# Cross-attention and mixture of experts in one kernel: the expert table and the zero blocks made in attention's block, four score banks in its drain, and other last sums and stores

## The reference

```python
x = x + tanh(g_xattn) * attention(layernorm(x), context)   # 16 heads of 16
x = x + tanh(g_ffn) * ffn(layernorm(x))

def ffn(x):                      # 12 experts, the top 3 of each row
    probs = softmax(x @ Wr + br)
    top_vals, top_idx = top_k(probs, 3)
    ew = softmax(top_vals)
    for e in range(12):
        sel = top_idx == e;  cnt = sel.sum()
        w_e = sum(where(sel, ew, 0)) / max(cnt, 1)
        h = relu(x @ w1[e] + b1[e]) @ w2[e] + b2[e]
        out = out + sel.any(-1)[..., None] * (w_e * h)
    phi = sigmoid(relu(out.mean(axis=1) @ Wp1 + bp1) @ Wp2 + bp2)
    return out * (1 - 0.8 * (phi > 0.7))
```

## Time and profile before

| | us |
|---|---|
| median of 3 timed runs | 2294.24 |
| lowest, highest | 2290.15, 2294.42 |
| the profiled execution | 2282.05 |
| its span, first to last instruction | 2280.3 |

### The profile page before, as it was taken

How to read it: one execution, slowest core, us unless ns; L and a number is a source line. 1 busy time by engine, 2 the same in 40 slices (tenths; PEclk the granted TensorE clock), 3 DMA queues, 4 the chain that set the end, 5 groups by cost and what they waited for, 6 DMA issues and landing times. The chain is left out here.

```text
span 2280.3 us, 61866 instructions
## 1 busy us (share of the span) xinstructions
PE 2146.6 (94%) x23534; PEld 1870.1 (82%) x23534; DVE 1414.3 (62%) x3219; ACT 1162.3 (51%) x2765; POOL 803.2 (35%) x1200
## 2 busy tenths in 40 slices
PE   5899999999999999999999999999993799999994
PEld 4688888888888888888888888888872678888883
DVE  4777777777777777777777777777743111111114
ACT  1366666666666666666666666666651223333330
POOL 4323433433433433443343343344211133333331
PEclk9999999999999999999999999999986899999996
DMA  5555555555555555555555555555403686777775
GB/s 137 146 132 151 138 139 138 134 148 137 132 137 139 146 139 141 134 139 144 136 131 139 150 134 144 134 135 137 125 19 104 209 270 187 218 220 218 210 222 158
DMA packets 253683, 345.06 MB, mean 151 GB/s; under 512 B 90280, under 2 KB 170508, under 8 KB 253260
## 3 DMA queue, kind: packets, MB, share of 16 engines
q1 hardware_dynamic: 222716, 304.93, 50.2%
q0 software_dynamic: 20256, 23.21, 5.2%
q10 hardware_dynamic: 10416, 12.98, 1.7%
HBM read 155.83 MB, written 42.86 MB: 87 GB/s over the span
## 5 line engine op out<-in xcount | busy, mean ns | idle before, releaser
L569 DVE TENSOR_REDUCE max_part<-max_ps 100x1 f32<-100x512 f32 (+1 forms) x1536 | 994.7, 655 | 349.2 <-PE max_ps L809 325.2
L452 ACT ACTIVATE probs<-score_ps 128x400 f32<-128x400 f32 (+1 forms) x1536 | 753.6, 503 | 427.6 <-PE score_ps L792 419.5
L792 PE MATMUL score_ps<-q_stack,k_stack 97*128 97x200 f32 (+1 forms) x3072 | 618.4, 284 | 4.6 <-ACT probs L452 3.4
L809 PE MATMUL max_ps<-k_stack,q_stack 96*100 96x512 f32 (+1 forms) x1536 | 597.2, 389 | 10.1 <-DVE max_part L569 9.6
L792 PEld LDWEIGHTS score_ps<-q_stack,k_stack 97*128 97x128 f32 (+1 forms) x3072 | 476.0, 184 | 78.0 <-issue 32.8
L389 POOL TENSOR_TENSOR ctx_hi<-ctx_raw,zero_col 128x256 fp32r<-128x256 f32 (+1 forms) x384 | 213.3, 586 | 467.7 <-PE v_ps L823 427.4
L859 PE MATMUL pv_ps<-probs,v_ones 128*17 128x100 f32 x12288 | 307.5, 253 | 0.6 <-ACT probs L452 0.6
L859 PEld LDWEIGHTS pv_ps<-probs,v_ones 128*17 128x17 f32 x12288 | 261.9, 99 | 45.1 <-issue 37.5
L809 PEld LDWEIGHTS max_ps<-k_stack,q_stack 96*100 96x100 f32 x1536 | 257.2, 167 | 21.6 <-DVE max_part L569 16.3
L1222 ACT ACTIVATE hid<-h_ps,b_c 128x256 f32<-128x256 f32 x245 | 116.0, 474 | 311.3 <-PE h_ps L1378 311.3
L1122 POOL DMA_INDIRECT results_by_token<-y_t,slot x98 | 152.9, 1561 | 343.1 <-DVE y_t L1329 185.3
(11 more groups left out here) (186 smaller groups left out, 2289.5 us busy)
## 6 DMA issues: line engine op xcount, KB each, us to landing
k_stack<-k_hl SPq DMA_DIRECT2D x512, 128.0 KB, 2.6
w_raw<-in_w SPq DMA_DIRECT2D x98, 640.0 KB, 5.2
ctx_raw<-in_ctxT SPq DMA_DIRECT2D x64, 512.0 KB, 4.5
k_stack<-k_hl SPq DMA_DIRECT2D x512, 64.0 KB, 2.2
k_stack<-k_hl SPq DMA_DIRECT2D x256, 105.0 KB, 2.5
ctx_raw<-in_ctxT SPq DMA_DIRECT2D x32, 420.0 KB, 4.8
k_stack<-k_hl SPq DMA_DIRECT2D x256, 52.5 KB, 2.0
x_t<-rows_by_expert SPq DMA_DIRECT2D x49, 269.0 KB, 4.8
```

The lines of the kernel that those rows point to most:

```text
L452: act.activation(probs[0:tw, n % PROBS, :], score_ps[n % 2][0:tw, 0:UH * SQ], ACT.Exp, scale=SCALE).then_inc(exp_done, 1)
L569: dve.tensor_reduce(max_part[b % 2][:, h, j:j + 1], max_ps[m % 2][0:SQ, 0:CW[j]], AX.X, ALU.max).then_inc(max_read, 1)
L792: ins = pe.matmul(score_ps[n % 2][0:TW[i], 2 * SQ * p:2 * SQ * (p + 1)], k_stack[b % 2][:, 2 * u + p, 128 * i:128 * i + TW[i]], q_stack[b ...
L809: pe.matmul(max_ps[m % 2][0:SQ, 0:CW[j]], q_stack[b % 3][0:96, h // 2, SQ * (h % 2):SQ * (h % 2) + SQ], k_stack[b % 2][0:96, h // 2, k0[j] ...
```

## The change

- In `attention`, POOL sets `zero_rows`, `ones_wide` and two rows of numbers in slot 378, in the room of `ctx_raw`, which is read no more by then.
- ACT issues the clear of `results_by_token` in slot 384 of attention.
- From score number 4 * 365 on (`WIDE` = 385 is its slot) the scores go round four banks, `v_ps` and `k_ps` being the other two, and wait for the exponential of n - 4. From tile 366 on (`SINGLE`) the values are multiplied tile by tile, 16 matmuls (32 instructions) in every slot.
- At the end of attention's lists PE makes the totals in `small_ps`; DVE adds `base` (the first row of each region) and writes the pads, and then the rest of the table and `wexp`, in the room of `probs`. SP and ACT issue six clears each as soon as the pads are there. SP waits for all clears before the block ends.
- `experts` begins with the load of the first rows and weights.
- In the tail DVE sums four of a part's five rows by two additions (2 x 512 wide to `pair_sum`, then 256), and PE takes the fifth row straight from `res` with a matmul pair of its own. A DVE step is folded into its neighbours: phi's last column is now -0.8 * (phi > 0.7), and factor is (sum + 1) * gate.
- Final products and stores go in pieces of 1, 2, 4, 6, 6 and 6 rows a partition, no longer five of 5.

```diff
+WIDE = NT * (B - 1) + 13
+SINGLE = NT * (B - 2) + 6
...
+def visit_of(tile):
+    return tile // 2 if tile < SINGLE else SINGLE // 2 + tile - SINGLE
...
+        def clear_pads(eng, some):
+            eng.wait_ge(pad_ready, 1)
+            for e in some:
+                row = eng.value_load(table[0:1, 3 * TILES + e:3 * TILES + e + 1], min_val=0,
+                                     max_val=NE * REGION - RT)
+                eng.dma_start(xs[bass.ds(row, RT), :].rearrange("(r p) d -> p r d", p=128),
+                              zero_rows.unsqueeze(1).broadcast_to([128, RT // 128, XW])).then_inc(cleared, 16)
+
+        drain_banks = [score_ps[0], score_ps[1], v_ps, k_ps]
+
+        def banks_of(n):
+            return 2 if n < UH * (WIDE - AT_SCORE) + 4 else 4
+
+        def score_bank(n):
+            return score_ps[n % 2] if n < UH * (WIDE - AT_SCORE) else drain_banks[n % 4]
...
+            clear_pads(sp, range(0, NE, 2))
             sp.wait_ge(x1_stored, 16 * B)
+            sp.wait_ge(cleared, 16 * NE)
+            sp.wait_ge(res_cleared, 16)
...
+                if g == NT * B - 6:
+                    pool.wait_ge(ctx_split, NC * B)
+                    pool.memset(zero_rows, 0.0).then_inc(tail_consts, 1)
+                    pool.memset(ones_wide, 1.0).then_inc(tail_consts, 1)
...
+                if g == NT * B:
+                    act.wait_ge(tail_consts, N_TAIL)
+                    act.dma_start(results, zero_rows[:, 0:D].unsqueeze(1).broadcast_to(
+                        [128, SLOTS // 128, D])).then_inc(res_cleared, 16)
+            clear_pads(act, range(1, NE, 2))
...
+            dve.wait_ge(totals_done, 1)
+            step(dve.tensor_copy(totals, small_ps[:, 0:2 * NE]))
+            step(dve.tensor_tensor(pad[0:SQ, :], base[:], totals[0:SQ, 0:NE], ALU.add))
+            dve.tensor_copy(table[0:SQ, 3 * TILES:], pad[0:SQ, :]).then_inc(pad_ready, 1)
...
-                wait(pe, exp_done, n + 1 - 2)
+                if n == UH * (WIDE - AT_SCORE):
+                    pe.wait_ge(v_read, NT * B)
+                    pe.wait_ge(k_read, KD * NC * B)
+                wait(pe, exp_done, n + 1 - banks_of(n))
...
-                if b is None or last % 2 == 0:
+                if b is None or (last % 2 == 0 and NT * b + last < SINGLE):
                     return
+                first = last - 1 if NT * b + last < SINGLE else last
...
-                for i in (last - 1, last):
+                for i in range(first, last + 1):
...
+            pe.matmul(small_ps[:, 0:2 * NE], ones_wide, counts[:], start=True, stop=True).then_inc(totals_done, 1)
...
-                dve.tensor_reduce(part_sum[:, i, :], res[0][:, pieces[i], :].rearrange("p i d -> p d i"), AX.X,
+                s = pieces[i].start
+                dve.tensor_tensor(pair_sum[:, i], res[0][:, s:s + 2, :], res[0][:, s + 2:s + 4, :],
+                                  ALU.add).then_inc(pair_ready, 1)
+                dve.wait_ge(pair_ready, i + 1)
+                dve.tensor_tensor(part_sum[:, i, :], pair_sum[:, i, 0, :], pair_sum[:, i, 1, :],
                                   ALU.add).then_inc(part_ready, 1)
...
             for i in range(PARTS):
+                pe.wait_ge(res_in[i], 16 * COPIES)
+                for k in range(KD):
+                    pe.matmul(pool_ps[:, k * B:k * B + B], res[0][:, pieces[i].stop - 1, 128 * k:128 * k + 128],
+                              of_batch[:], start=(i == 0 and k == 0), stop=False, skip_group_check=True)
                 pe.wait_ge(part_ready, i + 1)
```

More of the change, by code:

```diff
@@ L133, in attention @@
         slot_of = sb("slot_of", [SQ, TOPK, NE])
+        counts = sb("counts", [SQ, 2 * NE])
         half = sb("half", [SQ, 1])
@@ L150, in attention @@
         probs = sb("probs", [128, PROBS, UH * SQ])
+        room = probs[:].rearrange("p n q -> p (n q)")
+        totals, tmp, pad, ntiles, ends = (room[:, 32 * i:32 * i + n] for i, n in enumerate((2 * NE, NE, NE, NE, NE)))
+        t_exp, t_before, t_valid, t_row = (room[:, 192 + 64 * i:192 + 64 * i + TILES] for i in range(4))
+        more = room[:, 512:512 + NE * NCMP].rearrange("p (e c) -> p e c", e=NE)
+        past = room[:, 1024:1024 + TILES * NE].rearrange("p (t e) -> p t e", t=TILES)
+        skipped = room[:, 2048:2048 + TILES * NE].rearrange("p (t e) -> p t e", t=TILES)
         x_in = sb("x_in", [SQ, D])
@@ new lines, in _ @@
+            step(dve.tensor_reduce(ntiles, more, AX.X, ALU.add))
+            step(dve.tensor_tensor_scan(ends, ntiles, zero_rows[:, 0:NE], 0.0, ALU.add, ALU.add))
+            step(dve.tensor_tensor(past, wide(ends, [128, TILES, NE], 1), wide(tile_no, [128, TILES, NE], 2), ALU.is_le))
+            step(dve.tensor_tensor(skipped, past, wide(ntiles, [128, TILES, NE], 1), ALU.mult))
+            step(dve.tensor_reduce(t_exp, past, AX.X, ALU.add))
+            step(dve.tensor_reduce(t_before, skipped, AX.X, ALU.add))
@@ L941, in _, with experts @@
                         small_job(kind, b)
-def experts(nc, xs, ys, x1s, counts, g_ffn, w1, b1, w2, b2, wp1, bp1, wp2, bp2, out):
+            pe.wait_ge(small_read, len(SMALL_NO))
+            pe.wait_ge(counted, B + 1)
+            pe.wait_ge(tail_consts, N_TAIL)
+            pe.matmul(small_ps[:, 0:2 * NE], ones_wide, counts[:], start=True, stop=True).then_inc(totals_done, 1)
+def experts(nc, xs, ys, x1s, table, wexp, g_ffn, w1, b1, w2, b2, wp1, bp1, wp2, bp2, out):
     with ExitStack() as ctx:
@@ L1061, in experts @@
         pool_ps, mlp_ps, phi_ps, factor_ps = h_ps[0], h_ps[1], h_ps[2], h_ps[3]
+        outs = [slice(sum(STORES[:i]), sum(STORES[:i + 1])) for i in range(len(STORES))]
         pieces = [slice(TPP // PARTS * i, TPP // PARTS * (i + 1)) for i in range(PARTS)]
@@ L1133, in _ @@
         def _(sp):
-            sp.wait_ge(table_ready, 1)
-            sp.wait_ge(always, 1)
-            for e in range(NE):
-                row = sp.value_load(table[0:1, 3 * TILES + e:3 * TILES + e + 1], min_val=0,
-                                    max_val=NE * REGION - RT)
-                sp.dma_start(xs[bass.ds(row, RT), :].rearrange("(r p) d -> p r d", p=128),
-                             zero[:]).then_inc(cleared, 16)
-            sp.wait_ge(cleared, 16 * NE)
             def load_rows(t):
@@ L1355, in _ @@
         def _(pe):
-            pe.wait_ge(consts, 7)
-            pe.matmul(y_ps[0][:, 0:2 * NE], ones[:], counts[:], start=True, stop=True).then_inc(totals_done, 1)
+            pe.wait_ge(consts, 2)
             def transpose_x(t):
```

155 lines of the change are left out of this document (68 added, 87 removed).

## The result

The median went from 2294.33 us (2290.15 to 2295.13, 4 runs of the kernel before, one more than when the prediction was made) to 2267.78 us (2262.86 to 2269.99, 4 runs of the kernel after). The ratio is 0.9885, 95% interval 0.9868 to 0.9902: 26.5 us less. The forecast was 34.5 us less, 2260, range 2250 to 2275. The time lies in the range, 8 us above the forecast, between the times of rivals C (2264) and B (2270).

The account below looks back on a forecast made before the run. The time the change can touch was placed in three seams, with PE idle in the passage. Drain 13.5, passage 19.3 and tail 2.0 sum to 34.8, rounded to 34.5 off the 2294.24 median: 2259.7 us, range 2250 to 2275.

Parts of the forecast that it names:

- rival C: Passage from attention to experts: held by the clears, gaining 15 us instead of 19.3; time 2264, chance 0.12.
- Rival B: Drain of attention: clock stays or falls low again, gaining 2 to 5 us, not 13.5; time 2270, chance 0.22.
- signs of being wrong: Drain, passage, experts: clock of 0.5 past 1690, clears spaced over 1.5 us, or w_raw waits above 20 us.
- The term was 13.5 us: Drain of attention: four banks and smaller value groups save 13.5 us, bounds 2 and 15.5.
- The tile's 2.25 us: Drain at the high clock: 1.85 us of PE work plus 0.4 of waiting per tile of 128 keys.
- the clock comes back at 1681: Drain: after falling at neg_max the PE clock returns at 1681, not about 1695; 12.3 of 14 tiles then run at the high clock.
- The rule that was weighed: Drain: cycling through PSUM banks keeps the clock switching; the forecast went by the rows instead; if it held, Rival B.
- 19.3 forecast: Passage, attention to first expert product: PE starts at 1761.8 instead of 1781.16, 19.3 us less, bounds 15 to 22.
- full engines would give 340 GB/s: Passage: 235 GB/s at a share of 0.69 scales to 340, so 3.3 MB of clears take 9.7 us.
- The rule weighed there: Passage: DMAs from SP, ACT and GpSimd share 16 engines, so several issuers save only sequencer time; without it, 2.4 us better.
- 2.0 forecast: Tail: 2.0 us less, bounds 1.7 and 4.8 for the sums, with PE the last engine at 1.06 us per four instructions.
- rival E: Experts: weight loads land later, making the kernel slower; 1 us each in 49 turns gives 2308; chance 0.03.

Follow-up runs that it names:

- e1: Kernel after, unchanged, on the first follow-up chip: 2263.4 us, ratio 0.9877 to the kernel before.
- e2: Kernel before, unchanged, one profile on the same chip as e1: 2293.72 us.
- e3: Kernel after with the drain as before (two score banks, values multiplied by pairs of tiles): 2276.07 us, ratio 0.9934.
- e9: Kernel after, unchanged, on the third follow-up chip: 2249.03 us, ratio 0.9861 to the kernel before.
- e12: Kernel before, unchanged, one profile on the same chip as e9: 2283.13 us.
- e7: Kernel after with each clear writing two adjoining rows per partition as one 2152-byte piece, not two of 1076: 2245.74 us, ratio 0.9838.
- group 1: The runs e1 to e4, sharing one chip, where the kernel before ran in 2290.94 us (median of 7).
- e4: Kernel after with GpSimd's three scatters of batch 29 held until the exponentials of the last batch's second tile: 2259.58 us, ratio 0.9866.
- the first pair: First profiled runs of the unchanged kernels, before and after: 2282.05 and 2268.39 us.
- e6: Kernel after with all twelve clears on SP's queue, none on ACT's: 2248.1 us, ratio 0.9856.
- e5: Kernel after with batch 29's scatters held as in e4 and batch 30's until the last read-out: 2248.24 us, ratio 0.9849.

## Why the prediction was nearly right, point by point

The time lies in the range, but two of the three things that the prediction named as signs of being wrong were there in the first profile. The clock was at 0.50 past 1690 (1693.0 to 1706.6), and the clears of each queue were spaced over 1.5 us (1.7). The time stayed in the range since no term missed by more than some 3 us in the pairs on one chip, and the range is 25 us wide.

**Drain: mechanism right, clock wrong in detail, size right by two errors.** The term was 13.5 us. It measured 11.0 to 12.7 with ACT's long waits (e1 against e2, e3) and 16.7 without (e9 against e12), the last outside its bound of 15.5. The tile's 2.25 us was right (2.28). At the high clock the kernel before needs 5.49 us for a pair of tiles, so 14 tiles at 2.28 save (2.75 - 2.28) x 14 = 6.6 us; by this estimate the other 10 of e9's 16.7 are the clock, which e12 had low for much of its drain. The step that failed is "the clock comes back at 1681": it was worked out from the fall at neg_max in the earlier trace rows. With four banks there was no fall there in eight of ten traces. In e7 it fell (0.57 over 1676 to 1680) and was back within some 4 us, for 0.95 us of drain; in e1 it fell as well (0.75 over 1684 to 1688). The cold tiles were a charge for nothing in most runs: the forecast had 36.5 us from PE's neg_max to the end of the values, e9 shows 33.9. Against it stood what no row of the kernel before showed, an ACT that in one group of three takes up a finished bank some 2 us late. That the two nearly cancelled in group 1 (12.7 against 13.5) is luck.

Rival B expected the low clock from the way PE and ACT pass banks. It had the symptom for the first profile (0.50 over 1696 to 1704), not the reason: the fall came with one PE gap of 2.8 us, and e4 and e9 hold 1.00 with the same hand-over. The rule that was weighed, of the Trainium skill, "TensorE: Matmul & The Clock Gate", section "A second HAM failure mode: psum-queue depth-cycling", describes the kernel before: two banks, windows of 0.57 to 1.00 all through e12's drain. It doesn't describe the four-bank drain with groups of 32: seven of its ten traces hold 1.00 up to the last values, and the other three (the kernel after, e1, e7) fall near a PE gap of 1.1 or of 2.8 to 3.1 us.

**Read-out before the next values: not in the forecast.** In single visits the first values of the next batch come one tile after the old batch's last, and wait until ACT has copied pv_ps. That is 0.81 us in e9, and 2.8 to 3.1 where ACT is late. It is this dependence that turned ACT's delay into a gap of PE. The forecast compared two orders and didn't ask what the earlier visit waits for.

**The small jobs behind the drain: taken as unchanged.** They took 0.7 and 0.9 us more in the pairs on one chip and 3.8 in the first pair. The rows account for all three. In e1 against e2 ACT's read-out is 0.7 later (2.08 us behind the last values, 1.38 in e2). In e9 against e12 two PE jobs on `small_ps` run at a lower clock: 0.60 and 2.03 us for ones of 0.39 and 1.28, which is 0.96. In the first pair the read-out is 2.0 later, and four jobs take 1.06, 0.60, 2.03 and 0.57 for 0.61, 0.39, 1.11 and 0.36, which is 1.8. In these two pairs the clock of the kernel after is low soon after the last values (0.67 over 1708 to 1712 in e9, then 0.50), where the kernel before still has part of these jobs at the high one. Why it falls earlier there isn't shown.

**Passage: the term that was mis-sized.** 19.3 forecast, 16.0 and 16.2 measured, which is rival C. In e9 the chain up to the first clear was right (pads 2.0 us behind the counts where 1.6 was forecast, first clear 3.0 behind them against 3.1), the table was hidden, and x_t followed the next block's start by 0.7 where 1.1 was forecast. From the first clear to the next block's start it took 15.4 us, where 12.2 was forecast. From x_t to the first product it took 6.6 where the forecast took over the 6.0 of before: PE waits 2.58 us there for w_raw, 2.04 before, and why isn't shown. The step that failed is "full engines would give 340 GB/s". A share below one was scaled to one, at the pieces' unloaded cost. With two queues each piece of the clears occupies its engine longer. The DMA queues (packets, MB, share of the 16 engines' time) of e9 over 1725 to 1742,

```profile
q1 hardware_dynamic: 1632, 1.65, 35.3%
q10 hardware_dynamic: 1632, 1.65, 35.0%
```

of e6 over 1726 to 1744,

```profile
q1 hardware_dynamic: 3264, 3.31, 53.3%
```

and of e7 over 1726 to 1742:

```profile
q1 hardware_dynamic: 864, 1.65, 28.4%
q10 hardware_dynamic: 864, 1.65, 28.1%
```

In e9 that is 0.703 x 17 x 16 / 3264 = 59 ns a piece, in e6 47 ns, in e7 84 ns for a piece of nearly twice the bytes. These are means over all packets of the clears, 192 of which are not rows (3264 against 12 x 256). So a second queue lengthens the pieces by a quarter, and long pieces cost less for each byte. What it is behind the engine that limits them isn't shown. The rule weighed there, of the Trainium skill, "Trainium Kernel Development and Optimization", section "Key Constraints", was stronger than I let it be: the second queue bought 1.1 to 1.4 us.

**Tail: right engine, wrong rhythm.** 2.0 forecast, 3.2 in the trace. PE was to need 1.06 us a group, which is the length of one lone group in the earlier trace rows. Back to back they start 0.85 apart, since the last products of a group run beside the first of the next: ten groups in 9.0 us, and the parts' landing (1.58 us apart) is then almost as late. Three tiny steps of phi instead of four, and the stores, came out at +0.1 against 0.0.

**Experts: +0.2, +2.9, +2.7.** The forecast had nothing. The waits for w_raw grew a little: the first row below is of the kernel after (9.1 in the earlier trace rows), the others of e9 and e12. Without the first wait, which lies ahead of the first product (2.58 in e9, 1.96 in e12), e9 has 9.0 and e12 6.4, which is as much as the 2.7 between them; in e1 against e2 it is 8.5 against 7.1, half of the 2.9. So PE meets the weights a little later in these pairs, which is rival E in small. But the same stretch varies from 463.7 to 470.5 among the eleven traces with the new block order, and 2 us more in the mean (468.8 in the three of the unchanged kernel, 466.9 in the three of the kernel before) are not established as an effect of the change. It stays open.

```profile
PE h_ps L1424 <- DMA w_raw<-in_w: 9.9, 7, 6.2
...
PE h_ps L1424 <- DMA w_raw<-in_w: 11.6, 7, 6.2
...
PE h_ps L1378 <- DMA w_raw<-in_w: 8.4, 4, 6.0
```

**Why 8 us were missing** in the first measurement: by the pair e2 and e1, whose sum agrees with the timed runs, 2.5 in the drain (ACT's waits and the low clock), 3.1 in the passage, 0.7 in the small jobs, 2.9 in the experts, 0.3 ahead of the drain, less 1.3 that the tail gave more: 8.2. The 12.2 us between the profiled run of the kernel before and its median, which the prediction set aside, is probably of the same kind as the +8.4 of the first table: the last maxima are read at 1680.7 to 1685.3 in the four traces of group 1, and at 1672.9 to 1677.0 in the eight of the other two groups.

## What to carry to other kernels

A DMA rate at a share below one may not be scaled to a share of one when the transfers are of many pieces of about 1 KB: ask for the time of a piece under load, and make the pieces longer before adding a queue. The length of a lone group of matmuls is not the rhythm of such groups in a row. Before two seams a few microseconds wide are compared between two profiles, look at a stretch that the change cannot touch: if that differs, the pair is no pair.

## What the runs showed of the hardware

- ScalarE passed a finished PSUM bank about 2 us late at two places, each time while GpSimd issued its indirect scatters, in one group of runs of three: waits of 2.9 and 3.0 us marked "remote" (e1), and the first moved along when the scatters were moved (e4). In the kernel after, e1 and e4 the last read-out starts 0.15 us behind the start of the third scatter (1727.44 and 1727.29 in the first). It did not occur in seven traces of the other groups with or without the same scatters beside the same instructions. That the scatters cause it is suggested by this and not shown; the kernel with both groups held was not run on the chip that has the waits.
- Clears in 1076-byte rows from two queues moved 227 to 288 GB/s with the engines' share at 0.96 to 1.11 (kernel after), and 276 to 294 at 1.09 to 1.11 (e5); in 2152-byte pieces 380 and 391 at 1.06 and 1.05 (e7).
- A single gap of PE of 2.8 us in otherwise dense work came with 13.6 us at the low clock (1693.0 to 1706.6 in the kernel after), in nearly all of which PE worked without a gap; a gap of 3.1 us came with 6.8 us of it (1692.9 to 1699.7 in e1); the gap of about 1.1 us for neg_max was followed by no fall (e9), a short one (e7), or some 20 us of it (the kernel before, 1674.5 to 1695, where PE and ACT then also waited for each other).
